# Reordering the routed and shared tiles of a mixture-of-experts tail, with its loads and gathers

## The reference, cut to what matters

```python
h = layernorm(x) * (1 + cb) + sb                         # 4096 tokens x 128
probs = softmax(h @ w_router.T)                          # 8 experts
gates = the two largest probs of each token
shared = gelu(h @ Ws1.T + bs1) @ Ws2.T + bs2             # every token, hidden width 512
y_e = gelu(h @ W1[e].T + b1[e]) @ W2[e].T + b2[e]        # two experts per token, hidden width 512
x = x + gb * (shared + sum over e of gates[e] * y_e) / sqrt(1.25)
```

## Time and profile before

| what | before |
|---|---|
| median of three runs | 539.16 us |
| profiled execution, its own time | 532.91 us |
| its span, first to last instruction | 531.1 us |
| busy: TensorE, VectorE, ScalarE, GpSimd | 486.6, 390.8, 365.6, 349.4 us |
| TensorE's granted clock over the span | 0.971 of full speed |

### The profile page before, as it was taken

How to read it: one execution, slowest core, us unless ns; L and a number is a source line. 1 busy time by engine, 2 the same in 40 slices (tenths; PEclk the granted TensorE clock), 3 DMA queues, 4 the chain that set the end, 5 groups by cost and what they waited for, 6 DMA issues and landing times.

```text
span 531.1 us, 13354 instructions
## 1 busy us (share of the span) xinstructions
PE 486.6 (92%) x4030; PEld 442.3 (83%) x4030; DVE 390.8 (74%) x1613; ACT 365.6 (69%) x1383; POOL 349.4 (66%) x521
## 2 busy tenths in 40 slices
PE   3699999999999999999899979899989999899790
PEld 2489999999999999999747769789979998899680
DVE  4688888888898888988678887427885663343864
ACT  3369999899999999999759588554444544555450
POOL 4257767676776767775320788888888888776640
PEclk9579999999999999999998999999999999999997
DMA  9999900000000000000000114545447788698876
GB/s 194 332 397 393 354 3 1 2 1 3 2 2 2 2 2 2 2 2 2 1 2 0 43 42 134 182 120 172 129 134 217 244 269 260 215 286 265 329 231 184
DMA packets 39277, 68.50 MB, mean 129 GB/s; under 512 B 7475, under 2 KB 25781, under 8 KB 39205
## 3 DMA queue, kind: packets, MB, share of 16 engines
q1 hardware_dynamic: 31764, 56.69, 33.4%
q0 software_dynamic: 4320, 8.99, 4.8%
q10 hardware_dynamic: 3120, 1.97, 1.3%
HBM read 38.16 MB, written 29.46 MB: 127 GB/s over the span
## 4 chain that ended last, share of the span: by engine, by line
PE 62%; POOL 16%; issue 6%; DVE 6%; DMA 5%; ACT 3%; SPq 2%; another core or an unknown queue 1%; POOLq 0%; ACTq 0%; DVEq 0%
PE bank L1418 35%; POOL xs L1287 12%; PE bank L671 8%; PE bank L685 8%; POOL rested L1276 4%; DMA xr<-in_L_attn_x_dram 1%; PE bank L653 1%; DMA xt<-xs 1%; ACT hid L805 1%; DMA yg<-ys 1%; PE bank L566 1%; SPq L217 1%; PE bank L1627 1%; PE bank L1504 1%
## 5 line engine op out<-in xcount | busy, mean ns | idle before, releaser
L1295 POOL DMA_INDIRECT ys<-yo,dst x71 | 71.6, 1008 | 30.9 <-issue 15.2
L1287 POOL DMA_INDIRECT xs<-hrow,slot_i x64 | 62.9, 984 | 38.0 <-issue 38.0
L805 ACT ACTIVATE hid<-bank,slab 128x256 f32<-128x256 f32 (+1 forms) x172 | 62.6, 443 | 29.9 <-PE bank L671 23.0
L685 PE MATMUL bank<-slab,hid 128*128 128x128 f32 x568 | 71.9, 276 | 2.9 <-issue 1.6
L685 PEld LDWEIGHTS bank<-slab,hid 128*128 128x128 f32 x568 | 69.5, 192 | 5.4 <-issue 1.8
L671 PE MATMUL bank<-hg,slab 128*128 128x256 f32 (+1 forms) x344 | 68.8, 343 | 0.5 <-ACT hg L813 0.5
L671 PEld LDWEIGHTS bank<-hg,slab 128*128 128x128 f32 x344 | 55.0, 191 | 5.2 <-issue 0.7
L1174 DVE TENSOR_TENSOR yb<-bank,slab 128x256 f32<-128x256 f32 (+1 forms) x43 | 16.2, 378 | 56.2 <-PE bank L685 32.8
L813 ACT COPY hg<-bank 128x256 f32<-128x256 f32 (+1 forms) x43 | 14.4, 338 | 49.6 <-PE bank L653 34.4
L1276 POOL MEMSET rested<- 128x1408 f32 x32 | 41.3, 1290 | 0.0
L2311 POOL TENSOR_TENSOR nH<-aH,ones 128x128 f32<-128x128 f32 x32 | 14.9, 466 | 33.8 <-ACT aH L1767 33.8
(11 more groups left out here) (423 smaller groups left out, 1809.3 us busy)
## 6 DMA issues: line engine op xcount, KB each, us to landing
slab<-in_slabs_dram SPq DMA_DIRECT2D x43, 578.0 KB
xs<-fill SPq DMA_DIRECT2D x34, 528.0 KB, 7.6
xt<-xs SPq DMA_DIRECT2D x28, 132.0 KB
yg<-ys SPq DMA_DIRECT2D x7, 512.0 KB, 5.8
out_dram<-xr SPq DMA_DIRECT2D x18, 64.0 KB
ys<-yo,dst POOLq DMA_INDIRECT x71
xr<-in_L_attn_x_dram SPq DMA_DIRECT2D x4, 256.0 KB, 6.6
xs<-hrow,slot_i POOLq DMA_INDIRECT x64
```

Of the source, the lines that this page charges most:

```text
L685: mm = pe.matmul(y[:, s * D:(s + 1) * D], hid[i % 2][:, n, s * P:(s + 1) * P], right, start=(n == 0), stop=(n == FT - 1), skip_group_check ...
L805: nc.scalar.activation(hid[i % 2][:, n, 0:w], e_half(i, n)[:, 0:w], ACT.Gelu_apprx_tanh, bias=bias).then_inc(e_x, 1)
L1287: pool.indirect_dma_start(out=xs[:, :], out_offset=bass.IndirectOffsetOnAxis(ap=slot_i[:, i, c:c + 1], axis=0), in_=hrow[:, c, :], in_offs ...
L1295: pool.indirect_dma_start(out=ys[:, :], out_offset=bass.IndirectOffsetOnAxis(ap=dst[v][:, s:s + 1], axis=0), in_=yo[v][:, s, :], in_offset ...
```

## The change

The job list gets another order and another mix: 25 W and 21 H, still 71 blocks. Sixteen tiles now need only the first half of the tokens: the nine W, and seven H that are certain to be full once the nine are taken out (`FULL_HALVES`). They run ahead of the end of the dispatch with two shared tiles; before, nine W and five shared tiles stood there. Two shared tiles stand alone later in the list, and three are last; before, two were last. A new function `early_halves` makes the table of the seven, and `begin_rest` takes them out of what is left.

SyncE asks for the rows of a job two jobs ahead of its weights, and after the end of the dispatch it issues three loads of rows before the next weights. The rings `xt` and `yo` grow to 6 and 18. The loads of groups 0 to 3 and of 4 and 5 move from SyncE's queue to ScalarE's, behind the gelu of the fifth tile from the end and behind that of the first of the three last shared tiles. Of VectorE's 24 group operations fifteen stand between the last jobs and nine behind them; before, 18 and six. The early shared tiles write into the buffers `hid` of the jobs.

```diff
 N_FULL = -(-(B * S - E * (TS - 1)) // TS)
+FULL_HALVES = -(-(B * S - E * (P - 1)) // P) - SUB * N_FULL
+N_EARLY = N_FULL + FULL_HALVES
 EARLY_SH = 9
-N_WHOLE = (2 * B * S // P - E) // 2
-N_HALF = (2 * B * S + E * (P - 1)) // P - 2 * N_WHOLE
+N_REST = 16
+N_WHOLE = N_FULL + N_REST
+N_HALF = (2 * B * S + E * (P - 1)) // P - SUB * N_WHOLE
 N_TILES = N_WHOLE + N_HALF
-ORDER = "WW.WW.WW.WW.W." + "WWWW" + 6 * "WH" + 2 * "WWH" + "WWWWW" + "HHHHHHH" + ".."
+ORDER = "WW.WWWWHWHWHWHH.HH" + "WWW" + 4 * "WH" + "." + 4 * "WH" + "WWWWW" + "." + "HHHHHH" + "..."
...
-FIRST_HALF = WIDE.index(1)
+EARLY_HALF = WIDE.index(1)
+LATE_HALF = WIDE.index(1, N_EARLY)
+assert WIDE[:N_EARLY].count(SUB) == N_FULL and EARLY_HALF >= RW
...
+LEFT_HALF = (B * S + E * (P - 1)) // P - SUB * N_FULL - FULL_HALVES
+BY_HALF = covering(N_FULL + (LEFT_HALF + E) // SUB, FULL_HALVES + E)
+BY_THREE = covering(N_WHOLE, FULL_HALVES + E)
...
+RX = 6
+BIASED, BIAS_AT = EARLY_SH + 2, 19
+RY = 18
...
-        over = psb("over", [P, E, CAP // TS])
...
-        hs = [psb(f"hs{i}", [P, FT, SH]) for i in range(2)]
...
+        hs = hid
...
-            for j in range(N_FULL):
+            for j in range(N_EARLY):
+                if j == EARLY_HALF:
+                    sp.wait_ge(table_ready, 4)
                 rows(j)
                 if j >= RW:
                     weights(j)
-            sp.wait_ge(table_ready, 4)
-            weights(N_FULL)
-            weights(N_FULL + 1)
+            sp.wait_ge(table_ready, 6)
             sp.wait_ge(s_half[1], 16 * CH)
-            for j in range(N_FULL, N_TILES):
-                rows(j)
-                if j == FIRST_HALF - 1:
-                    sp.wait_ge(table_ready, 6)
-                if j >= N_FULL + 2:
-                    weights(j)
-                if j == LOAD_AT:
-                    scattered(sp, BY_HALF)
-                if LOAD_AT <= j < LOAD_AT + 4:
-                    load(sp, j - LOAD_AT)
-            scattered(sp, BY_THREE)
-            load(sp, 4)
-            load(sp, 5)
+            rows(N_EARLY)
+            rows(N_EARLY + 1)
+            for j in range(N_EARLY, N_TILES):
+                if j + 2 == LATE_HALF:
+                    sp.wait_ge(table_ready, 8)
+                if j + 2 < N_TILES:
+                    rows(j + 2)
+                weights(j)
             store(sp, 0)
-            store(sp, 2)
             scattered(sp, N_TILES)
...
+                if i == job["expert", N_TILES - 5]:
+                    scattered(act, BY_HALF)
+                    for g in range(4):
+                        load(act, g)
+                elif i == len(JOBS) - 3:
+                    scattered(act, BY_THREE)
+                    load(act, 4)
+                    load(act, 5)
...
+                then(dve.scalar_tensor_tensor(out=over[:, :, :], in0=held[:, 0, :].unsqueeze(2).broadcast_to(grid),
+                                              scalar=-float(P - 1), in1=cut["step"].unsqueeze(1).broadcast_to(grid),
                                               op0=ALU.add, op1=ALU.is_gt))
-                then(dve.tensor_reduce(full[:, :], over[:, 0:E, :], AX_X, ALU.add))
+                then(dve.tensor_reduce(full[:, :], over[:, :, :].rearrange("p e (k o) -> p e k o", o=2)[:, :, :, 1], AX_X, ALU.add))
...
+            def early_halves():
+                seen = past[:, 0:N, :]
+                then(dve.tensor_reduce(full_by[:, :], over[:, :, :], AX_X, ALU.add))
+                then(dve.tensor_scalar(begun[:, :], marks[:, 0:E], float(SUB), None, ALU.mult))
+                then(dve.tensor_tensor(full[:, :], full_by[:, :], begun[:, :], ALU.subtract))
...
+                then(dve.tensor_reduce(etab[:, early], seen, AX_X, ALU.add))
+                dve.tensor_scalar(e_i[:, early], etab[:, early], float(E - 1), None, ALU.min).then_inc(table_ready, 1)
...
+                dve.wait_ge(table_ready, 3)
+                dve.tensor_copy(row_i[:, early], rowf[:, early]).then_inc(table_ready, 1)
+
+            def begin_rest():
+                then(dve.tensor_scalar(last[:, 0, :], last[:, 0, :], float(N), None, ALU.min))
+                then(dve.tensor_tensor(begun[:, 1:E], begun[:, 1:E], last[:, 0, 1:E], ALU.add))
+                then(dve.tensor_tensor(begun[:, 1:E], begun[:, 1:E], last[:, 0, 0:E - 1], ALU.subtract))
+                then(dve.tensor_tensor(begun[:, 0:1], begun[:, 0:1], last[:, 0, 0:1], ALU.add))
+                then(dve.tensor_scalar(marks[:, 0:E], begun[:, :], 1.0 / SUB, None, ALU.mult))
+                then(dve.scalar_tensor_tensor(out=left[:, :, :], in0=begun[:, :].unsqueeze(1).broadcast_to([P, 3, E]), scalar=-float(P),
...
+                then(dve.tensor_tensor(each(marks[:, E:4 * E]), each(marks[:, E:4 * E]),
+                                       marks[:, 0:E].unsqueeze(1).broadcast_to([P, 3, E]), ALU.add))
+                then(dve.tensor_tensor(each(units[:, :]), each(units[:, :]), begun[:, :].unsqueeze(1).broadcast_to([P, 3, E]), ALU.add))
...
+            SUMS = {-6: (0,), -5: (1,), -4: (2, 3, 4), -3: (5, 6, 7, 8, 9), -2: (10, 11, 12, 13, 14)}
...
+                dve.wait_ge(sh_ready, min(BIASED, (g + 1) * GRP // SUB))
...
+                    if j >= BIASED:
...
+                if i == 0:
+                    early_halves()
+                elif i == 1:
+                    begin_rest()
+                elif i == 3:
                     rest_marks()
-                elif i == 3:
+                elif i == 4:
                     ends(marks)
-                elif i == 5:
+                elif i == 6:
                     experts_of(rest, n_rest)
-                elif i == 6:
-                    rows_at(rest, n_rest, marks, TS, 3)
                 elif i == 8:
+                    rows_at(rest, n_rest, marks, TS, 5)
+                elif i == 9:
                     half_marks()
-                elif i == 9:
+                elif i == 10:
                     ends(marksh)
-                elif i == 11:
-                    experts_of(halves, N_HALF)
                 elif i == 12:
-                    rows_at(halves, N_HALF, marksh, P, 5)
-                elif N_FULL + 6 <= i < N_FULL + 6 + NG:
-                    shared_bias(i - N_FULL - 6)
+                    experts_of(halves, N_HALF - N)
+                elif i == 13:
+                    rows_at(halves, N_HALF - N, marksh, P, 7)
+                elif BIAS_AT <= i < BIAS_AT + NG:
+                    shared_bias(i - BIAS_AT)
                 for k in SUMS.get(i - len(JOBS), ()):
                     group_step(k)
-            group_step(17)
             dve.wait_ge(sh_ready, N_SH)
-            for k in range(18, 24):
+            for k in range(15, 24):
                 group_step(k)
```

More of the change, by code:

```diff
@@ L34 @@
 N_SH = B * S // SH
+RW = 5
 PARTS = ((0, 2), (2, 4), (4, 6), (6, 8))
@@ L412, in program @@
         held, marks = psb("held", [P, 3, E]), psb("marks", [P, 4 * E])
-        over = psb("over", [P, E, CAP // TS])
+        over = psb("over", [P, E, CAP // P])
         tri = psb("tri", [P, 3 * E, E])
         odd, units, clipped = (psb(n, [P, 3 * E]) for n in ("odd", "units", "clipped"))
+        full_by, begun, left = psb("full_by", [P, E]), psb("begun", [P, E]), psb("left", [P, 3, E])
         run, marksh = psb("run", [P, E]), psb("marksh", [P, 4 * E])
@@ L1071, in rest_marks @@
                 dve.wait_ge(turned, NG)
-                then(dve.tensor_tensor(over_all, held[:, :, :].rearrange("p k e -> p (k e)").unsqueeze(2).broadcast_to(grid),
+                then(dve.tensor_tensor(over_all, left[:, :, :].rearrange("p k e -> p (k e)").unsqueeze(2).broadcast_to(grid),
                                        cut["step"].unsqueeze(1).broadcast_to(grid), ALU.is_gt))
@@ L1167, in e_post @@
                     dve.wait_ge(e_yb, i + 1)
-                    if j >= EARLY_SH + 5:
+                    if j >= BIASED:
                         dve.wait_ge(xs_ready, NG)
```

34 lines of the change are left out of this document (19 added, 15 removed).

## The result

The changed kernel took 550.59 us in the median of four runs (546.08 to 551.22), the kernel before 540.38 beside it: a ratio of 1.0218, interval 1.0167 to 1.027. It is slower by 2.2%. The forecast was 536.6, and 550.6 lies above its whole range. The profiled execution took 550.14 us with a span of 548.3, against 532.91 and 531.1: 17.2 us of span, more than the 10.2 between the medians, since before's profile shows one of its better runs and after's an ordinary one.

A forecast was written before the change was run, and what follows sets the result against it. Bounds: GpSimd's dispatch until 391, then TensorE's chain, with 12.0 us of waits. Work 157.7 plus waits 3.0 + 3.0 + 1.0 + 1.0 = 8.0 gave T = 515.2, end 528.55 (-2.55): 536.6 us, range 529.5 to 542.5.

The forecast's parts named there:

- The early term: Around the dispatch's end, TensorE waits for VectorE and late weights together: 3.0 us, bounds 0 and 7.5.
- the next weights: After three row loads, weights leave at 399.29 and land at 404.8, wanted at 402.3; lateness bounds 0 and 2.5 us.
- 0.3 us of issue each: In SyncE's queue, each row load moves ahead of two weights waits at 0.3 us of issue each, nothing else behind it.
- three more loads of weights: In TensorE's work, six H for three W cost nothing in multiplication, only three more weight loads; work is +0.2 us.
- VectorE's hold: In the early list VectorE is full, 47.9 of 48.6 us, so any hold shows; TensorE waits 0 to some 5.6 us.
- the reading for eight memsets: By the lockout rule, each early GpSimd memset could cost VectorE 1.29 us, 10.3 in all, putting early waits at their upper bound.
- The group loads: Four loads in ScalarE's queue take about 0.4 us of issue each between gelus of an H: 1.0 us, bounds 0 and 2.
- rival C: Gathers share DMA engines with the last weights; the run of H keeps its 5.2 us: 540.8 us, chance 0.14.
- The wait at the dispatch's end: TensorE's wait there for rows, 1.8 us and its restart, goes because more jobs precede it: -2.0 us.
- The middle waits: Four waits between 438 and 465 stay, untouched by the change: 3.0 us with restarts, bounds 0 and 3.5.
- The row waits in the run of H: With rows two jobs ahead, waits of 4.5 us and 0.7 of restarts shrink to 1.0, bounds 0 and 5.2.
- The tail: Behind TensorE's last matmul T, VectorE rather than the gather is last; end at T + 13.35, so +1.25 us.

The follow-up runs named there:

- later_weights_first: Changed kernel with group loads two tiles later and, in the late loop, a tile's weights issued ahead of the rows two tiles on: 537.76 us, ratio 1.0031.
- five_shared_sync: Changed kernel with five shared jobs early and two last, weights ahead of rows in the late loop, groups 0 to 5 loaded ending SyncE's loop: 539.03 us, ratio 1.0033.
- weights_ahead: Changed kernel with the weights of tiles 16 and 17 issued before SyncE waits for the end of the dispatch: 550.07 us, ratio 1.0255.
- rows_from_scalar: Changed kernel with group loads two tiles later and the rows of tiles 6 to 15 asked for from ScalarE's queue: 546.24 us, ratio 1.0147.
- groups_later: Changed kernel with the four group loads on ScalarE's queue two tiles later, behind the last tile's weights: 545.96 us, ratio 1.0188.
- late_loads_scalar: Kernel before with one more shared tile last instead of early, rows two jobs ahead, late group loads from ScalarE's queue, sums as in the change: 543.04 us, ratio 1.0078.
- before_vector_24: Kernel before with 24 more small chained VectorE operations behind jobs 0, 1 and 2: 539.37 us, ratio 1.0003.

## Why the prediction was wrong

**The early term: 3.0 us forecast, 10.1 and 2.9 of half clock measured.** The step that failed is "the next weights": the forecast had tile 16's leaving at 399.3 and there at 404.8, against 402.3 when TensorE wants them, and bounded the lateness by 2.5. They left at 413.00 and landed at 415.82. So the landing, 2.82 us for 5.5 assumed, was faster than forecast, and all of the loss is in the leaving: 13.7 us later than forecast, 9.9 if both are counted from the first job. The forecast took SyncE's time after the dispatch from before, where SyncE stood idle at that wait, and never asked whether it would be there in time. SyncE's queue:

```profile
378.38 0.01 SPq L526 DMA_DIRECT2D slab<-in_slabs_dram  x1
...
389.17 0.32 SPq L526 DMA_DIRECT2D slab<-in_slabs_dram  x1
...
401.80 0.32 SPq L526 DMA_DIRECT2D slab<-in_slabs_dram  x1
...
405.12 0.71 SPq L526 DMA_DIRECT2D slab<-in_slabs_dram  x1
408.07 3.45 SPq L533 DMA_DIRECT2D xt<-xs  x3
413.00 0.00 SPq L526 DMA_DIRECT2D slab<-in_slabs_dram  x1
```

From the weights at 378.38 to those at 405.12 are seven pairs of rows and weights in 26.7 us, 3.8 each, with 0.4 us of waiting for VectorE in all of them. TensorE takes a W and an H in 5.63, one tile in 2.8. So in the part of alternating W and H SyncE falls back by about 1 us a tile, and it reached its wait for the dispatch at 405.87, some ten microseconds after that was met. "0.3 us of issue each" was the length of the DMA instruction in the row; around it stand two or three register steps, and 26 pieces of the chain between 380.98 and 413 last about 0.7 us or more. The forecast had the six H for three W cost "three more loads of weights" and gave these no price. At this place it is more than three: SyncE issues sixteen tiles ahead of the end of the dispatch where before it issued the rows of nine and the weights of eleven, and two shared tiles instead of five stand between them.

The runs show what mends it. The order of the issues, with the group loads out of the way, takes away the wait for tile 16's weights and leaves the 6.4 us of small ones ahead of it (later_weights_first); more time without loads in the early list, with that order, takes away both (five_shared_sync). Moving two loads at one place does neither (weights_ahead). That SyncE's pace is the whole cause is not shown: relieved of rows alone it stood for VectorE instead (rows_from_scalar), and in after it stood 10.3 us in four waits for VectorE's results between 355 and 381, the last of them, 0.4, on the chain and behind table operations.

**VectorE's hold** was the other half of that term. TensorE waited for no result of VectorE between 353 and 413. In kind it was right twice over: the hold at a small operation is there,

```profile
362.89 1.47 DVE L1089 TENSOR_SCALAR rowf<-rowf,begun 128x7 f32<-128x7 f32 x1
```

(1.47 us, where small ones take 0.18 in the earlier trace rows; GpSimd's memset stands from 363.04 to 364.32), and once SyncE is relieved VectorE is next (rows_from_scalar). The Trainium skill (SBUF — State Buffer, "Who interferes with whom") gives the lockout with GpSimd as a whole instruction, and single holds of 1.33, 1.47 and 1.77 us, each across a memset of 1.3, agree; the reading for eight memsets, 10.3 us and an early term at its upper bound by VectorE, did not come about. Nor was VectorE full: the forecast's 47.9 of 48.6 us stand against 38.5 busy of 50 in 355 to 405, 0.77 and not above 0.9, and it was busy 28.26 us of 349.5 to 391.5 against 28.54 in the earlier trace rows.

**The group loads: 1.0 us forecast, 3.76 of wait and 1.8 of half clock measured.** The term priced the issue on ScalarE alone and put what the loads do to SyncE's at nothing. The step that failed is in rival C: "only the weights of the very last tile are issued after them now". That one is enough. ScalarE's queue, the four loads:

```profile
510.27 0.34 ACTq L479 DMA_DIRECT2D yg<-ys  x1
510.64 1.43 ACTq L479 DMA_DIRECT2D yg<-ys  x3
```

The weights, 578 KB, leave at 511.87 behind these 2 MB and land 8.29 us later, where tile 16's took 2.82. C's mechanism, gathers and last weights on the same DMA engines, was right, but it stood as one case of four, not as a term beside the early one; that its 5.2 us are close to the end's loss is luck, as they were waits for rows that went. The rule cited there, from the Trainium skill (DMA: Bandwidth & Descriptors, "Issuing engines are not separate DMA queues"), has its first half shown now: loads from ScalarE's queue held up one from SyncE's. That issue time alone is saved no run shows. Two tiles later the loads cost none of it (groups_later, 6.7 us less). The other two waits of the end, 0.64 and 0.67, are not the loads': the first stands ahead of them, and groups_later has two like them.

**Half clock** had no term at all: 6.4 us of the 24.3. Each long wait of this trace (3.55, 1.98, 3.76) is followed by a stretch at 1.2 GHz, by the means above 7.0, 3.6 and 3.5 us, so a wait cost up to twice what it says. It need not: in before the longest wait was 2.50 us in the run of H, and the clock stayed at 1.00 behind it.

**Right.** The wait at the dispatch's end is gone. The middle waits stay, 1.98 us at 441.22 for 3.0 forecast. The row waits in the run of H are gone, but the run as a whole is no faster: it stands from 504 to 523 in after, and with the wait for the last weights in it TensorE is busy 13.9 us of 19, against 14.5 in the earlier trace rows. GpSimd is no limit, its scatters are starved:

```profile
L1342 POOL DMA_INDIRECT ys<-yo,dst x71 | 69.6, 980 | 44.4 <-DVE gt L1198 19.0 <-issue 16.3 <-DVE yo L1223 9.2
```

The tail was forecast at T + 13.35 with VectorE as its end; it is T + 12.96, and VectorE is busy 13.00 of the 13.5 us from 532. The work stands as well: from the first up multiplication to T TensorE is busy 167.5 us, 161.1 without the 6.4 of half clock, and 160.4 in before. Two terms of the sum were wrong, both for what stands behind an instruction in a queue, and both carried their loss on as half clock.

**Open.** Why SyncE's register steps take 0.7 us at some times and 0.01 to 0.3 at others was not tried, nor how much of tile 16's lateness is VectorE's from before 381. Nor is it settled whether group loads from ScalarE's queue cost anything by themselves when they come late enough. And why the middle wait near 441 is there in most kernels was left alone.

## What to carry to other kernels

When an order asks for more tiles in the same time, add up the queue that issues their loads as one adds up an engine: the interval between two issues in the trace, with its register steps, against the time that the consumer takes for a tile. Where a queue holds several kinds of loads, put first what is wanted first, and let no wait for a later job's address stand ahead of an earlier job's data. Before bulk loads are moved to another engine's queue, look at which small load is issued just after them, and count a stall of TensorE with the slower clock that may follow it.

## What the runs showed of the hardware

- A pair of loads, one of 132 KB or 66 KB at a row read from a table and one of 578 KB, took SyncE 2.3 to 3.3 us where it waited for nothing (413.00, 415.75, 418.07, 421.38 in after), and 3.8 us between 378 and 405, where it waited 0.4 in all, though the DMA instructions themselves show 0.0 to 0.7.
- TensorE ran at half clock in work as well as after waits. From 280 to 320 us, ahead of the job list, its mean clock was 0.96 in before, 0.87 in after and 0.74 in late_loads_scalar, though it was busy 36 to 38 of the 40 us in each; the list started at 348.4, 352.4 and 358.8. Comparing job lists rather than spans took most of that out of the profiles, not out of the timed runs, which spread by 1% on either side.
- Waits of 1.98, 3.55 and 3.76 us (after) and 3.61 (before_vector_24, mean clock 0.71 from 506 to 516) had half clock behind them; one of 2.50 us (before) had none.
- The same 578 KB took 2.82 us to land with little beside it and 8.29 behind four loads of 512 KB, which took 6.0 in the median (DMA share 0.86 from 511.87 to 520.16).
